# Edge stages that turn their own rows: a graph-attention kernel without its stored turned copy

## The reference

```python
xn = _layernorm(x, axis=-1)                      # (x - mean) / sqrt(var + eps)
# graph attention, twice; per edge (src -> dst), 8 heads of 32
alpha = leaky_relu(a_src[src] + a_dst[dst] + a_edge, 0.2)
ex    = exp(alpha - segment_max(alpha, dst)[dst])
out   = segment_sum(xp[src] * (ex / (denom[dst] + 1e-16))[:, :, None], dst) + bias
# the mix, on xn
q, k, v = split(xn @ W_qkv + b_qkv);  q -= mean(q);  k -= mean(k)
k2 = l2_normalize(k*k / (sum(k*k) + 1e-7), over nodes)
q2 = l2_normalize(q*q / (sum(q*q) + 1e-7), over features)
attn = v + (q2 @ (k2.T @ v)) / sqrt(6250)
x = x + graph(xn) + (attn @ W_out + b_out)[nodes]
x = x + experts(_layernorm(x))
```

## Time and profile before

| | us |
|---|---|
| runs of the kernel before | 3036.64, 3046.49, 3049.08 |
| their median | 3046.49 |
| the profiled execution | 3039.37 |
| its span, first to last instruction | 3037.6 |
| first stage | 0 to about 112 |
| edge stage of layer 0 | about 118 to 1205 |
| edge stage of layer 1 | about 1315 to 2403 |
| PE / DVE / ACT / POOL busy | 2343 / 2164 / 1172 / 1995 |
| granted TensorE clock, mean of the span | 0.886 of full speed |

### The profile page before, as it was taken

The page is one execution under the profiler, slowest core; times in us unless marked ns, Lnnn a source line. Parts: engine busy times, 40 slices in busy tenths (PEclk is TensorE's granted clock), DMA queues, the critical chain, the costliest instruction groups (busy, mean ns, idle before and its releaser), DMA issues. The chain is left out here.

```text
span 3037.6 us, 76113 instructions
## 1 busy us (share of the span) xinstructions
PE 2343.2 (77%) x15555; PEld 1937.5 (64%) x15556; DVE 2164.0 (71%) x6024; ACT 1172.0 (39%) x4767; POOL 1995.0 (66%) x2241
## 2 busy tenths in 40 slices
PE   6587878888888887847777777777777757499897
PEld 4466667676666666636666666666666536378786
DVE  7477878787877786647777778777787655666565
ACT  3244545444444444513333333333333442322222
POOL 4577777777777774577777777777777225166665
PEclk9799989999999999859988989898888857699999
DMA  9755655565555553256566556655555248444432
GB/s 255 207 169 156 172 157 166 166 171 160 166 168 168 157 167 86 86 146 180 159 178 175 168 169 175 176 167 173 172 169 167 62 140 271 121 160 152 122 116 86
DMA packets 295113, 484.48 MB, mean 159 GB/s; under 512 B 69669, under 2 KB 204989, under 8 KB 295045
## 3 DMA queue, kind: packets, MB, share of 16 engines
q0 software_dynamic: 96384, 286.92, 33.3%
q1 hardware_dynamic: 134340, 150.23, 17.1%
q10 hardware_dynamic: 64320, 46.56, 4.9%
HBM read 404.17 MB, written 81.43 MB: 160 GB/s over the span
## 5 line engine op out<-in xcount | busy, mean ns | idle before, releaser
L703 POOL DMA_INDIRECT e_rows<-table,e_idx x1664 | 1580.2, 950 | 557.1 <-issue 403.4
L1087 PE MATMUL e_ps_sum<-e_hot,e_msg 128*128 128x129 f32 x6656 | 1118.6, 306 | 267.3 <-DVE e_msg L744 210.6
L1087 PEld LDWEIGHTS e_ps_sum<-e_hot,e_msg 128*128 128x128 f32 x6656 | 920.9, 205 | 427.0 <-ACT parts L942 242.2
L941 ACT ACTIVATE acc<-e_ps_sum 128x256 f32 x1664 | 639.0, 384 | 1222.8 <-PE e_ps_sum L1087 1022.7
L744 DVE TENSOR_TENSOR e_msg<-e_rows,e_ps_pr 128x256 f32<-128x256 f32 x1664 | 654.6, 415 | 82.0 <-issue 12.9
L723 DVE TENSOR_TENSOR e_hot<-e_ps_pr,rel 128x512 f32<-128x512 f32 x416 | 285.4, 686 | 163.2 <-PE e_ps_sum L1087 157.7
L1069 PE MATMUL e_ps_al<-e_dst_score,e_hotT 128*128 x3328 | 301.6, 180 | 1.5 <-issue 0.7
L1069 PEld LDWEIGHTS e_ps_al<-e_dst_score,e_hotT 128*128 128x128 bf16 x3328 | 251.5, 99 | 60.1 <-issue 2.3
L942 ACT ACTIVATE parts<-e_ps_sum 128x4 f32 (+1 forms) x1664 | 280.4, 168 | 0.0
L1076 PE MATMUL e_ps_al<-ident,e_lr 128*128 128x128 f32 x104 | 38.6, 371 | 171.8 <-DVE e_lr L768 170.8
L2010 ACT ACTIVATE x_h<-x,eb 128x128 f32<-128x128 f32 x216 | 67.4, 363 | 260.8 <-PE x L2079 260.8
(11 more groups left out here) (319 smaller groups left out, 3400.4 us busy)
## 6 DMA issues: line engine op xcount, KB each, us to landing
e_relb<-rel_rows SPq DMA_DIRECT2D x104, 512.0 KB
e_rows<-table,e_idx POOLq DMA_INDIRECT x1664
e_eattr<-in_edge_b SPq DMA_DIRECT2D x104, 128.0 KB
e_xT<-turned_x ACTq DMA_DIRECT2D x100, 128.0 KB
e_xr<-in_x ACTq DMA_DIRECT2D x100, 128.0 KB
node<-acc SPq DMA_DIRECT2D x25, 512.0 KB, 3.8
table<-t_row SPq DMA_DIRECT2D x25, 276.0 KB, 4.1
table<-j_row SPq DMA_DIRECT2D x25, 276.0 KB, 2.5
```

What stands on the lines that cost most here:

```text
L703: nc.gpsimd.indirect_dma_start(out=rows[q][:, k, :], out_offset=None, in_=table, in_offset=bass.IndirectOffsetOnAxis(ap=idx[:, q, k:k + 1] ...
L941: nc.scalar.activation(acc[:, :, bass.ds(at[k], P)], ps_sum[(k + q) % 3][:, :, 0:P], ACT.Copy).then_inc(s["window"], 1)
L1087: op = nc.tensor.matmul(ps_sum[(k + q) % 3][:, a, 0:WIN], msg[:, k % RM, a * P:a * P + P], hot[:, q, k, :], start=(a == 0), stop=True, ski ...
```

## The change

The first stage no longer copies and stores the turned norms. Each edge stage centres the rows of its block itself (ScalarE, with `negm`), transposes the centred rows on PE and copies them out of PSUM on ScalarE; the missing factor `rstd`, one number per node, is applied to the product's rows by VectorE, in the instruction that adds the bias (layer 0) or the raw rows (layer 1). Since the centring now comes ahead of the keys, it moves from k = 8 to k = 6, the block's loads from k = 6 to k = 7, the keys from k = 8 to k = 9, `keys_centred` from k = 10 to 11 and the squares from k = 11 to 12. In layer 1 the centring of the next block stands at k = 14, its transposes beside those of `q2` at k = 0, and one copy of 512 columns takes both out.

```diff
 first, SP
-                sp.wait_ge(s["copied"], n + 1)
-                sp.dma_start(turned_x[n], xnT[:, n % 2]).then_inc(s[f"xo{n % 2}"], 16)
 first, ScalarE
-                nc.scalar.activation(xnT[:, n % 2], turn[n % 2][:].rearrange("p (a n) -> p a n", a=2), ACT.Copy
-                                     ).then_inc(s["copied"], 1)
...
 edges, VectorE
             def keys_centred(g):

                 vec.wait_ge(s["kq"], g + 1)
-                nc.vector.tensor_tensor(kq[:], ps_a[:], bkq[:], ALU.add).then_inc(s["kqc"], 1)
+                nc.vector.scalar_tensor_tensor(kq[:], ps_a[:], rstd[:, bass.ds(g, 1)], bkq[:], ALU.mult, ALU.add
+                                               ).then_inc(s["kqc"], 1)
...
-                nc.vector.tensor_tensor(base[:, q], ps_b[:, 0:F], xr[:, q], ALU.add)
+                nc.vector.scalar_tensor_tensor(base[:, q], ps_b[:, 0:F], rstd[:, bass.ds(g, 1)], xr[:, q], ALU.mult, ALU.add)
...
                     if block_too and layer == 0:
-                        if k == 10:
+                        if k == 11:
                             keys_centred(g)
...
 edges, ScalarE
             def fetch_block(g, q, i):

                 if not isinstance(g, int) or g >= 2:
-                    act.wait_ge(s["kq" if layer == 0 else "base"], g - 1 if layer == 0 else g)
-                    if layer == 0:
-                        act.wait_ge(s["xc"], g)
-                act.dma_start(xT[:, q], turned_x[bass.ds(i, 1), :, :, q * P:q * P + P].rearrange("a p b n -> (a p) b n")
-                             ).then_inc(s[f"xT{q}"], 16)
+                    act.wait_ge(s["xc" if layer == 0 else "base"], g)
                 act.dma_start(xr[:, q], x[bass.ds(g * P, P), :]).then_inc(s[f"x{q}"], 16)
...
                 act.wait_ge(s[f"x{q}"], 16 * i + 16)
-                act.wait_ge(s["kx"], g + 1)
+                act.wait_ge(s["kx" if layer == 0 else "q2T"], g + 1)
                 nc.scalar.activation(xc[:], xr[:, q], ACT.Identity, bias=negm[:, bass.ds(g, 1)]).then_inc(s["xc"], 1)
...
-            def squares_turned(g):
-                act.wait_ge(s["q2T"], g + 1)
-                nc.scalar.activation(q2T[:], ps_a[:, 0:2 * P].rearrange("p (a n) -> p a n", a=2), ACT.Copy).then_inc(s["q2c"], 1)
+            def rows_turned(g):
+                act.wait_ge(s["xcT"], g + 1)
+                nc.scalar.activation(xcT[:], ps_a[:, 2 * P:4 * P].rearrange("p (a n) -> p a n", a=2), ACT.Copy).then_inc(s["xcTc"], 1)
+
+            def block_turned(g):
+                act.wait_ge(s["q2T"], g + 2)
+                nc.scalar.activation(turned[:], ps_a[:].rearrange("p (a n) -> p a n", a=4), ACT.Copy).then_inc(s["q2c"], 1)
...
                     if block_too and layer == 0:
+                        if k == 6:
+                            rows_centred(g, q, i)
                         if k == 8:
-                            rows_centred(g, q, i)
-                        if k == 11:
+                            rows_turned(g)
+                        if k == 12:
                             block_squares(g, q, i)
                     if block_too and layer == 1 and k == 4:
-                        squares_turned(g)
-                    if block_too and k == 6:
+                        block_turned(g)
+                    if layer == 1 and k == 14 and (not isinstance(g, int) or g + 1 < NB):
+                        rows_centred(g + 1, 1 - q, i + q)
+                    if block_too and k == 7:
                         if not isinstance(g, int) or g + 1 < NB:
                             fetch_block(g + 1, 1 - q, i + q)
...
 edges, PE
-            def keys(g, q, i):
-
-                pe.wait_ge(s[f"xT{q}"], 16 * i + 16)
+            def turn_rows(g):
+                pe.wait_ge(s["xc"], g + 2)
                 pe.wait_ge(s["cols"], g + 1)
                 for a in range(2):
-                    op = nc.tensor.matmul(ps_a[:], xT[:, q, a, :], wkq[:, a, :], start=(a == 0), stop=(a == 1))
+                    op = nc.tensor.transpose(ps_a[:, (2 + a) * P:(3 + a) * P], xc[:, a * P:a * P + P], ident[:])
+                op.then_inc(s["xcT"], 1)
+
+            def keys(g):
+                pe.wait_ge(s["xcTc"], g + 1)
+                for a in range(2):
+                    op = nc.tensor.matmul(ps_a[:], xcT[:, a, :], wkq[:, a, :], start=(a == 0), stop=(a == 1))
                 op.then_inc(s["kq"], 1)
...
-            def turn_squares(g, q, i):
+            def turn_block(g, q, i):
                 pe.wait_ge(s[f"q2{q}"], 16 * i + 16)
+                pe.wait_ge(s["xc"], g + 1)
                 pe.wait_ge(s["q2c"], g + 1)
                 for a in range(2):
-                    op = nc.tensor.transpose(ps_a[:, a * P:a * P + P], q2[:, q, a * P:a * P + P], ident[:])
+                    nc.tensor.transpose(ps_a[:, a * P:a * P + P], q2[:, q, a * P:a * P + P], ident[:])
+                for a in range(2):
+                    op = nc.tensor.transpose(ps_a[:, (2 + a) * P:(3 + a) * P], xc[:, a * P:a * P + P], ident[:])
                 op.then_inc(s["q2T"], 1)
...
                     total(g, q, k)
...
-                    if block_too and layer == 0 and k == 8:
-                        keys(g, q, i)
+                    if block_too and layer == 0:
+                        if k == 6:
+                            turn_rows(g)
+                        if k == 9:
+                            keys(g)
...
                     if softmax and k == 6:
                         turn_alpha(n)
```

37 lines of the change are left out of this document (16 added, 21 removed).

## The result

| | us |
|---|---|
| before, median of 4 runs of the comparison | 3043.43 (3036.64 to 3049.08) |
| changed kernel, median of 4 runs | 3188.52 (3181.62 to 3190.17) |
| ratio, with its 95% interval | 1.0465 [1.0449, 1.0481] |
| predicted | 3073 (range 3028 to 3130) |
| profiled execution of the changed kernel, its span | 3188.72, 3186.9 |

What follows compares the result with a forecast made beforehand. POOL's gathers were taken to set the pace, with the compute engines close behind in layer 0. From 3039.4 us, +41 for layer 0, 0 for layer 1 and -8 for the first stage gave 3073 us, range 3028 to 3130.

Steps and rivals of the forecast that it cites:

- the ring: VectorE, PE and ScalarE working in turn behind POOL's gathers; in layer 0 said to need 19.8 of 20.4 us a step.
- hand-over: Layer 0, tile 6: PE waits for ScalarE's centred rows and transposes them before the scores; 1.38 us a step.
- the mean of 1.38: Mean delay in us of turn_alpha over 39 layer 0 steps (0.90 to 1.71), taken as the cost per step.
- the lower bound named for it: Layer 0: the delay of the scores costs nothing if VectorE's next wait on PE, at one_hots, gives it all back.
- `keys_centred` at 0.07: Layer 0: its longer instruction form, 128x512, adds 0.07 us a step on VectorE, bounds 0 and 0.14.
- the copy at 0: Layer 0: ScalarE's 0.392 us copy of xcT beside tile 9's sum; 0 to 0.3 us sticks out, taken as 0.
- The clock: Layer 0: PE's new 1.2 us pause lies at the edge of slow key products; no extra cost taken as likeliest.
- clock falls in every step: Rival, layer 0: the 1.2 us pause slows PE each step, +112 us, 3143 with the first stage; 13%.
- nothing to gain: First stage: removing 25 ScalarE copies of 0.60 us saves nothing, since PE is fully busy from 95 us on.
- cover enough: Layer 0: ScalarE, busy 497 of 1,051 us, absorbs one DMA issue fewer and a 0.392 us copy of xcT.
- Layer 1: Second edge stage: added work under 0.7 us a step against 1.4 us of waiting for rows; 0, bounds 0 and +5.
- First stage: Stage before the edge stages: removing five stores while DMA is saturated gives -8 us, bounds 0 and -20.

Runs made afterwards that it cites:

- before_turns: Kernel before with two unused transposes of the identity matrix on PE at tile 6 of layer 0, ahead of turn_alpha: 3040.5 us, ratio 0.9995.
- best: Changed kernel with rows centred one step ahead, turn_alpha first, copy at tile 7, keys at 8, keys_centred 10, squares 11, 26 no-effect ScalarE instructions: 3040.3 us.
- before_pause: Kernel before with layer 0's centring at tile 6 and two unused PE transposes of the centred rows there, ahead of turn_alpha: 3047.1 us, ratio 1.0016.
- rows_ahead_padded: Changed kernel with layer 0's rows centred one step ahead into two buffers, and 26 no-effect instructions at the start of ScalarE's program: 3040.8 us.
- after_padded: Changed kernel with 26 no-effect instructions added at the start of ScalarE's program: 3069.8 us, ratio 1.0101.
- before_shifted: Kernel before with 226 no-effect instructions added at the start of ScalarE's program: 3051.3 us, ratio 1.0031.
- before_pause_shifted: Kernel before with the edits of before_pause and before_shifted together: 3203.0 us, ratio 1.0535.
- the padded runs: Changed kernel with 13, 26 or 256 no-effect instructions at the start of ScalarE's program: 3071.9, 3069.8 and 3194.4 us.
- after_filled: Changed kernel with six unused transposes of the identity matrix on PE at tile 0 of every second step of layer 0: 3127.5 us, ratio 1.0269.
- after_by_13: Changed kernel with 13 no-effect instructions added at the start of ScalarE's program: 3071.9 us, ratio 1.0095.

## Why the prediction was wrong, point by point

**What bounds the kernel: right.** POOL sets the pace, the ring has 32.5 us in hand in layer 0. Every kernel that stays inside that (before_turns, best) takes 1062 to 1065 us there, and the waits for rows are what is used up first. It helps to count the ring's demand as growth of layer 0 plus the waits that vanished:

| edit | layer 0 | + waits eaten | = ring |
|---|---|---|---|
| hand-over alone (before_pause) | 10.2 | 28.2 | 38 |
| the other edits, no hand-over (rows_ahead_padded) | 6.7 | 9.3 | 16 |
| all edits, no stall (after_padded) | 34.5 | 29.5 | 64 |
| stall alone (before_shifted) | 2.3 | 24.0 | 26 |
| hand-over and stall (before_pause_shifted) | 159.6 | 29.0 | 189 |
| changed kernel | 143.0 | 27.4 | 170 |

**Layer 0, the hand-over: the mechanism right, the price near.** The forecast had (1.38 + 0.07) x 51 = 74 us on the ring, +41 on the layer. `after_padded` has 64 and +34.5, with a wait of 1.21 us on PE where 1.2 was forecast. The parts are less good than the sum, and that the sum comes out so near is in part luck. The hand-over alone is 38 us, half of the 70 that the mean of 1.38 gives; the lower bound named for it (given back at later waits) is partly real. The other edits cost the ring 16 us (the two transposes ahead of the scores among them), where `keys_centred` at 0.07 and the copy at 0 made 4: the keys at tile 9 are waited for (`e_kq` 28.0 us in rows_ahead_padded, 16.4 before), which I had argued away with "VectorE also picks the result up one tile later".

**The clock: the wrong trigger.** I had read out of the trace that a wait of 1.15 us or more on PE came with slow keys in all of 11 blocks, and took the wait for the cause. `before_pause` puts 1.2 us of waiting at that place into each step, and the granted clock is 0.98. So the wait by itself does not bring the clock down; what did in those 11 steps was not tried. The section of the Trainium skill cited in the prediction ("TensorE: Matmul & The Clock Gate", "HAM oscillation — how this bites in real kernels") has long pauses as the cause, and for the wait at tile 6 the run agrees with it. For the stand of 1.29 us behind ScalarE's stall the trace does not: the rows at 862 show 0.51 for the next 14 us. So the length of one pause does not decide it, and the rival "clock falls in every step" came nearest to the measured time (3143 against 3188.5) for a reason that was not there: its sign was key products of 3.3 us in most steps, and in 30 of the 50 blocks of the changed kernel they take 1.95 to 1.98 us, in the other 20 2.6 to 3.8.

**The step that failed** is the costing of what leaves ScalarE: in the first stage the 25 copies are "nothing to gain", in layer 0 one DMA issue fewer is "cover enough". They were counted as time and not as instructions in a program. Taking 27 of ScalarE's instructions out ahead of the loop (356 against 329) moved it across a boundary and cost 119 us (3188.5 against 3069.8), the whole of the miss: without it the kernel takes 3069.8, and 3073 was forecast. No row of the trace of before shows this. The loop's position can be counted in both compiled programs without a run; that it decides over the stall is what the padded runs showed. What the trace did show is how little the ring could take: 32.5 us in hand against two burdens of 26 and 38, which alone fit or nearly fit, and together do not. Behind that point the loss seems to feed on itself (a late PE waits, its clock falls, it is later still); `after_filled` shows the part of the clock in it, the circle as such is only argued.

**Layer 1:** +9.1 us, forecast 0 to +5. 8.6 of it lie in POOL's seven pauses, 28.0 us in sum over the normal spacing (19.4 before, and 18.5 in `after_padded`, whose layer 1 is 1059.4). The waits for rows are still 76.2 us. Since `after_padded` has the same edits there, no cost of them is to be seen. **First stage:** -6.5 us in this pair, forecast -8. `before_pause` and `before_turns`, whose first stage is that of before, start their first gather at 115.6 and 116.7 us; the kernels with the new first stage and at most 26 added instructions start it at 111.1 to 113.8. So the gain is nearer 5 us.

**What the profile was to show:** the wait of 1.2 us on PE, `e_peak` over 1 us in each step, waits for rows nearly gone and gaps throughout held; "about 1,100 instead of 1,062 us" held only in `after_padded` (1096.3) and `after_by_13` (1094.9).

## What to carry to other kernels

An edit that removes instructions can cost time far behind the place where it stands, if it moves a long loop across a block boundary of its engine's program; so count the loop's position in both kernels, and when a layer is slower than its parts explain, look at the first instruction behind each jump and at the packets of the instruction queue. Costs that eat the same slack do not add: price them together against it, and take any sum that goes beyond it as a lower bound. And a correlation of waits with a low clock in one trace doesn't say which caused which: a wait put in by hand takes one run.

## What the runs showed of the hardware

- A jump back of ScalarE's loop (280 to 286 instructions, two steps) stands 3.9 to 4.9 us before the next window where the loop's start lies at 70 to 75 modulo 256 in its program, and 1.6 to 2.2 us at 86 to 101. With the long stand the instruction queue moves 118 packets (0.97 MB) in layer 0, without it 8 (0.07 MB). Layer 1's loop of some 260 instructions does not stall in any of these kernels.
- 226 added instructions that only wait, at the start of ScalarE's program, put the first gather at 126.7 to 130.9 us in three kernels, where it is at 115.6 to 119.7 in three without them: some 11 us, or 50 ns each, by the means.
- Giving PE 144 needless transposes during its stand made the kernel 61 us faster by the medians (33 in the profiled executions, where the time at the lower clock, by the estimate above, fell from 286 to 186 us).
- A wait of 1.2 us of PE in each 20 us step, with two transposes behind it, leaves the granted clock at 0.98, above the 0.94 of the kernel without them and the 0.95 with the transposes alone. I have no explanation for the rise.
